# Moving the next tile's preparation two steps later inside a scan tile, in a graph network with a Mamba block

## The chip, the cores and the metric

One NeuronCore of a Trainium2 chip. Time is device microseconds of one execution of the program. TensorE multiplies matrices, VectorE, ScalarE and GpSimd do elementwise work, SyncE (SP) only issues transfers.

## The reference

With x [4096, 128] and adj [4096, 4096], all float32:

```
stage A:  for (x1, W1), (x2, W2):  h = (2 + eps) * (adj @ x_k);  three times h = relu(h @ W.T + b)
          x = layernorm(x + concat(h1, h2) @ Wm.T + bm)
stage B:  g = relu(adj @ x @ gcn_w + gcn_b);  h = layernorm(g) * ln_g + ln_b
          xc, z = split(h @ w_in);  u = silu(causal_conv(xc, 4 taps) + conv_b)
          dt_low, B, C = split(u @ w_xp);  dt = softplus(dt_low @ w_dt + b_dt)
          scan over 4096 rows, 16 states of 256 channels:  hs = exp(dt*A) * hs + dt*u*B
          y = (sum over states of hs*C + u*D) * silu(z);  out = layernorm(x + y @ w_out)
```

## The kernel before

Rows are worked in eight tiles of 512. Stage A transposes adj, multiplies it, and stores the transposed tiles 1 to 7 in HBM (`adjT`). Stage B reads them back in chunks of four 128-column blocks (`adjc`, four buffers) and multiplies each block with x: 32 "adj products" a tile, summed in one PSUM bank (`accB`), each of two instructions.

Stage B has one **window** for each tile b. A window has 16 turns, here **steps**, one for each state n. All five engines run the same steps from their own queues, written out by hand, and meet only through semaphores. In a window three things are interleaved: the scans of tile b, the **front** of tile b+1 (all that must be ready before its scans), and the **tail** of tile b−1 (gate, output projection, layernorm). Besides, TensorE works on the adj products of a tile ahead.

The scan work of step n. TensorE: spread B n+1 and spread C n−1 (a row of B or C over all partitions, in PSUM), and `sum_state(n-3)`, which adds eight transposed blocks of pr. VectorE: dBuV n (even n, L946, reads a PSUM bank), scan n−1 (L960, reads dA and dBu in SBUF), pr n−2 (L967, hs times a PSUM bank). GpSimd: dBuP n for odd n (L507, `POOL`); it waits for scan n−3 (`POOL_AFTER`), and product 1 waits for `dtu` of its tile. ScalarE: copy of a state, two dA (L714, it may be four scans ahead), the starting value of scan n−1 (L724), which the scan waits for.

The front of a tile, in order: axT (`front_ax`, ScalarE, L625); gcn (`front_gcn`, TensorE, L1123); relu (ScalarE); transpose (`front_gtr`); the statistics (`front_g`, VectorE, L886 to L895); rs and nb (`front_rs`, GpSimd, L490 and L492, tiny); hn (ScalarE, L636); transpose (`front_tr`); hT (ScalarE); eight conv products (`front_xc`, TensorE, L1143, four to each of two banks); u and sz (`front_silu`, ScalarE, L651 and L654, with a load of the activation table before and after), where sz waits for z (`front_z`, TensorE, L1152) and z for u; dbc (TensorE); bc (`front_bc`, ScalarE) and its low part `bclo` (`front_bclo`, VectorE, L900); dt product; `sp` (ScalarE), `spd`, `sp_r`, `dt` and `dtu` (VectorE, L904 to L917).

The tables at L39 to L53 say in which step of its engine each part stands: `AT` by name, `CONV` the conv products and `PLAN` the adj products of TensorE's steps, `FILL` the products that stand between the parts of front 0 before the first window, here the **gap**. `step_of` adds 1 to 16 of the names in window 0, which has no tail. Window 7 has no front, and the adj products of the kernel before end with window 5. SP issues the chunk loads in order; each waits until the chunk four before it has been multiplied. The functions that the change touches:

Of the kernel before, what the change touches and what calls it, by code (L numbers as in the profile page):

```python
# [25 lines left out]
S = 16  # L26
# [5 lines left out]
def wait(eng, sem, value):  # L32

    if not isinstance(value, int) or value > 0:
# [1 line left out]

AT = dict(pool_rs=3, pool_tail_rs=13, dve_dt=14, act_hn=4, act_hT=5, act_silu=9, act_bc=11,  # L39
          act_sp=12, act_exp=13, act_tail=14, dve_g=1, dve_bc=9, dve_sp=12, dve_gate=1, dve_tail=11, pe_tr=3,  # L40
          pe_z=7, pe_dbc=8, pe_dt=10, pe_turn=2, pe_out=9, act_b0=14, act_b1=2, act_b2=5, act_b3=9, act_ax=15, act_g=0, act_start=1, act_skip=2, act_y=4)
SHIFTED = ("pool_rs", "act_hn", "act_hT", "act_silu", "act_bc", "act_sp", "act_exp", "act_b0", "dve_g", "dve_bc", "dve_sp",
           "dve_dt", "pe_tr", "pe_z", "pe_dbc", "pe_dt")


def step_of(name, tail):

    return AT[name] + (0 if tail or name not in SHIFTED else 1)


FILL = (1, 1, 6, 1, 0, 0, 2, 9, 12)
CONV = (0, 0, 0, 0, 3, 3, 2, 0, 0, 0, 0, 0, 0, 0, 0, 0)
PLAN = (2, 4, 4, 1, 1, 0, 2, 1, 2, 1, 1, 3, 3, 2, 3, 2)  # L53
C_IN_O = (0, 2, 4, 6)
POOL = (1, 3, 5, 7, 9, 11, 13, 15)
POOL_AFTER = 3
# [4 lines left out]
def gnn_mamba(nc, x, adj, x2, eps1, eps2, W1, b1, W2, b2, Wm, bm, gcn_w, gcn_b, ln_g, ln_b, w_in, conv_w,  # L61
# [3 lines left out]
    with ctx:  # L65
# [319 lines left out]
        def _(pool):  # L385
# [114 lines left out]
            def window(b, par, tail, front):  # L500
                for n in range(S):
                    if n in POOL_B:
                        pair = nB(n) // 2
                        pool.wait_ge(b_in[pair % 2], 16 * (NPB // 4 * b + pair // 2 + 1))
                        wait(pool, scanned, S * b + (n - POOL_AFTER if n >= POOL_AFTER else -1) + 1)
                        pool.wait_ge(dtu_ready, b + 1)
                        nc.gpsimd.tensor_tensor(dBu(n, par)[:, :, 1:], dtu[par][:, :, :],  # L507
                                                b_sb[pair % 2][:, nB(n) % 2:nB(n) % 2 + 1, :].to_broadcast([P, H, TILE]),
                                                ALU.mult).then_inc(dBu_by_pool, 1)
                    if front and n == step_of('pool_rs', tail):  # L510
                        front_rs(b + 1)
                    if tail and n == AT['pool_tail_rs']:
                        tail_rs(b - 1)
# [16 lines left out]
        def _(act):  # L530
# [91 lines left out]
            def front_ax(a):  # L622
                act.wait_ge(ax1_summed, a + 1)
                wait(act, gcn_product, a)
                nc.scalar.activation(axT[:, :], accB[:, :], ACT.Copy).then_inc(ax1_ready, 1)  # L625
# [73 lines left out]
                act.dma_start(b_sb[pair % 2][:, :, :], rows_[2 * pair:2 * pair + 2, :].partition_broadcast(P))\  # L699
                    .then_inc(b_in[pair % 2], 16)  # L700

            def window(b, par, tail, front, adj_):
                for n in range(S + (0 if front else LAG)):
                    k = n - LAG
                    if k >= 0 or tail:
# [18 lines left out]
                        nc.scalar.activation(dBu(k, par)[:, :, 0], state[:, k, :], ACT.Copy).then_inc(start_set, 1)  # L724
                    if n in (AT['act_b1'], AT['act_b2'], AT['act_b3']):
                        load_B(b, par, 1 + (AT['act_b1'], AT['act_b2'], AT['act_b3']).index(n))
                    if adj_ and n == AT['act_ax']:
                        front_ax(b + 2)
                    if front:
                        if n == 1 and not tail:  # L730
                            front_ax(b + 1)
                        if n == (AT['act_g'] if tail else 2):
                            front_relu(b + 1)
                        if n == step_of('act_hn', tail):
                            front_hn(b + 1)
                        if n == step_of('act_hT', tail):
                            front_hT(b + 1)
                        if n == step_of('act_silu', tail):
                            front_silu(b + 1, 1 - par)
                        if n == step_of('act_bc', tail):  # L740
                            front_bc(b + 1, 1 - par)
                        if n == step_of('act_sp', tail):
                            front_sp(b + 1, 1 - par, 0)
                        if n == step_of('act_exp', tail):
                            front_sp(b + 1, 1 - par, 1)
                        if n == step_of('act_b0', tail):
                            load_B(b + 1, 1 - par, 0)
                    if n == AT['act_skip']:
                        skip_term(b, par)
# [20 lines left out]
            front_sp(0, 0, 0)  # L770
            front_sp(0, 0, 1)
            load_B(0, 0, 0)
            window(0, 0, False, True, True)
            window(1, 1, True, True, True)
            with act.Fori(0, 2) as i:
                window(2 * i + 2, 0, True, True, True)
                window(2 * i + 3, 1, True, True, True)
            window(6, 0, True, True, False)
            window(7, 1, True, False, False)
            tail_copy(TILES - 1)  # L780
            tail_norm(TILES - 1)

# [2 lines left out]
        def _(dve):  # L785
# [153 lines left out]
            def window(b, par, tail, front):  # L939
                for n in range(S + 2):  # L940
# [29 lines left out]
                    if tail and n == AT['dve_gate']:  # L970
                        tail_gate(b - 1, 1 - par)
                    if front:
                        if n == step_of('dve_g', tail):
                            front_g(b + 1)
                        if n == step_of('dve_bc', tail):
                            front_bclo(b + 1, 1 - par)
                        if n == step_of('dve_sp', tail):
                            front_spd(b + 1, 1 - par)
                        if 0 <= n - step_of('dve_dt', tail) < 3:
                            front_dt(b + 1, 1 - par, n - step_of('dve_dt', tail))  # L980
                    if tail:
                        if n == AT['dve_tail']:
                            tail_stats(b - 1, 1 - par)
# [23 lines left out]
        def _(pe):  # L1007
# [112 lines left out]
            def front_gcn(a):  # L1120
                pe.wait_ge(ax1_ready, a + 1)
                wait(pe, sp_abs_relu, 4 * a)
                mm(M0[:, :], gcn_w_sb[:, :], axT[:, :], start=True, stop=True).then_inc(gcn_product, 1)  # L1123
# [13 lines left out]
            def front_xc(a, j0, j1):  # L1137

                for j in range(j0, j1):
                    h, k = j // TAPS, j % TAPS  # L1140
                    if j == 0:
                        pe.wait_ge(h_ready, a + 1)
                    last = mm((M0, M1)[h][:, :], w_cv_sb[:, h, k, :], hT[:, k:k + TILE], start=(k == 0), stop=(k == TAPS - 1))  # L1143
                    if k == TAPS - 1:
                        last.then_inc(conv_summed, 1)
# [73 lines left out]
            def tail_out(b, par, groups, then):  # L1219
# [10 lines left out]
                if groups[-1] == RG - 1:  # L1230
                    last.then_inc(projected, 1)

            def window(b, par, tail, front, adj_):
                for n in range(S + 1):
                    if n % 2 and n + 1 < S:
                        spread_B(b, n + 1, par)
                    if tail and n == 0:
                        for k in LATE:
                            sum_state(b - 1, k)
                    if front and not tail and n == 1:  # L1240
                        front_gcn(b + 1)
                    if front and n == (0 if tail else 2):
                        front_gtr(b + 1)
                    if n == step_of('pe_tr', tail):
                        if adj_:
                            adj_blocks(b + 2, sum(PLAN[:n]), sum(PLAN[:n + 1]))
                        if front:
                            front_tr(b + 1)
                    if n == SUM_AFTER:
                        sum_skip(b)  # L1250
                    if n >= SUM_AFTER:
                        sum_state(b, n - SUM_AFTER)
                    if tail and 0 <= n - AT['pe_out'] < 2:
                        half = RG // 2 * (n - AT['pe_out'])
                        tail_out(b - 1, 1 - par, range(half, half + RG // 2), True)
                    if adj_ and n < S and n != step_of('pe_tr', tail):
                        adj_blocks(b + 2, sum(PLAN[:n]), sum(PLAN[:n + 1]))
                    if front:
                        k = n if tail else n - 1
                        front_xc(b + 1, sum(CONV[:max(k, 0)]), sum(CONV[:k + 1]))  # L1260
                        if n == step_of('pe_z', tail):
                            front_z(b + 1, 0)
                            front_z(b + 1, 1)
                        if n == step_of('pe_dbc', tail):
                            front_dbc(b + 1, 1 - par)
                        if n == step_of('pe_dt', tail):
                            front_dtp(b + 1, 1 - par)
                    if tail and n == AT['pe_turn']:
                        tail_turn(b - 1)
                    if adj_ and n == S:  # L1270
                        front_gcn(b + 2)
                    if n > 0:
                        spread_C(b, n - 1, par)
                    if front and n == S:
                        spread_B(b + 1, 0, 1 - par)
# [63 lines left out]
```

## Time and profile before

| | |
|---|---|
| median of 3 runs | 1144.08 us (1141.78 to 1144.95) |
| the profiled execution | 1143.51 us, its span 1141.6 us |
| busy share: TensorE, VectorE, ScalarE, GpSimd | 86%, 91%, 46%, 26% |
| mean granted TensorE clock | 0.957 |
| stage A | to about 490 us |
| gap | about 490 to 540 us |
| windows: scan 0 starts at | 529.87, 612.23, 686.97, 761.80, 836.66, 910.21, 984.2, 1057.65 us |
| last scan | 1118.7 us |

Busy is the time in which an engine had an instruction under way. A duration is that of one instruction; engines overlap the end of one with the start of the next, so that the distance of two starts is the better price of an instruction in a full queue.

### The profile page before, as it was taken

The page shows a single profiled execution, that of the slowest core. Times are in us where ns is not written, and L with a number is a line of the kernel's source. Part 1 is how long each engine was busy: PE and PEld are TensorE (multiplying, and loading weights), DVE is VectorE, ACT ScalarE, POOL GpSimd, SP SyncE. Part 2 cuts the span into 40 slices and gives each one's busy share as a digit, 9 for nine tenths or more (in the row PEclk, how much of TensorE's full clock was granted, in tenths as well). Part 3 has the DMA queues.
Part 4 walks back from the last instruction along what each step waited for, and adds up shares of the span by engine and source line. Part 5 has one row for each costly group of instructions (what it writes and reads, how often), then busy time and mean ns, then how long its engine had stood idle before and what let it go on. Part 6 is the DMA issues. An engine that isn't in the chain of part 4 may idle for free. (4 is left out here: it accounts for less than half of the span.)

```text
span 1141.6 us, 13185 instructions
## 1 busy us (share of the span) xinstructions
PE 984.3 (86%) x4162; PEld 677.3 (59%) x4162; DVE 1036.0 (91%) x858; ACT 527.2 (46%) x946; POOL 295.3 (26%) x197
## 2 busy tenths in 40 slices
PE   0689999999999999999988979979889799685555
PEld 0567777777777877444555646646556465463444
DVE  1999999999999999724999999999999999999994
ACT  1343343434444342324555555736456556564431
POOL 5321112020202110102323224332333243322340
PEclk9999999999999999999999999999999999896776
DMA  9999999999999999847444253254441542101100
GB/s 263 225 178 304 332 330 347 322 349 326 326 355 321 352 329 310 189 180 257 159 158 166 94 203 133 72 207 146 164 182 61 202 147 75 38 20 55 38 9 10
DMA packets 190908, 226.37 MB, mean 198 GB/s; under 512 B 8624, under 2 KB 164336, under 8 KB 176528
## 3 DMA queue, kind: packets, MB, share of 16 engines
q1 hardware_dynamic: 105920, 163.60, 43.9%
q10 hardware_dynamic: 81856, 54.80, 18.8%
q0 software_dynamic: 3088, 7.47, 2.1%
q8 instruction: 18, 0.29, 0.1%
q14 instruction: 26, 0.21, 0.1%
HBM read 162.66 MB, written 63.18 MB: 198 GB/s over the span
## 5 line engine op out<-in xcount | busy, mean ns | idle before, releaser
L807 DVE STREAM_TRANSPOSE at<-rows 128x1024 f32<-128x1024 f32 x136 | 267.7, 2009 | 21.6 <-DMA rows<-in_adj 8.4
L507 POOL TENSOR_TENSOR dBuP<-dtu,b_sb 128x1024 f32<-128x1024 f32 x64 | 153.5, 2398 | 397.5 <-DVE hs L960 227.5
L1025 PE MATMUL yT<-ah,xh 128*128 128x512 f32 x512 | 211.1, 412 | 47.8 <-DVE al L815 42.7
L547 ACT ACTIVATE ah<-at 128x2048 fp32r<-128x2048 f32 x64 | 122.5, 1915 | 210.2 <-PE yT L1025 208.6
L1112 PE MATMUL bank<-adjc,xm 128*128 128x512 f32 x448 | 210.7, 599 | 1.6 <-ACT axT L625 1.6
L1025 PE MATMUL yT<-ah,xl 128*128 128x512 f32 x512 | 200.5, 392 | 0.0
L1025 PE MATMUL yT<-al,xh 128*128 128x512 f32 x512 | 200.5, 392 | 0.0
L1196 PE MATMUL yT<-ident,pr 128*128 128x128 f32 x1024 | 152.5, 299 | 38.0 <-DVE pr L967 38.0
L714 ACT ACTIVATE dA<-dt,A_sb 128x512 f32<-128x512 f32 x256 | 169.7, 713 | 26.2 <-DVE dt L914 26.0
L1196 PEld LDWEIGHTS yT<-ident,pr 128*128 128x128 f32 x1024 | 132.2, 154 | 65.0 <-DVE pr L967 51.4
L967 DVE TENSOR_TENSOR pr<-hs,bank 128x1024 f32<-128x1024 f32 x128 | 153.0, 1196 | 3.9 <-PE bank L1192 3.8
L960 DVE TENSOR_TENSOR_SCAN hs<-dA,zero,dBuP 128x1026 f32<-128x1026 f32 x64 | 154.8, 2419 | 0.0
L960 DVE TENSOR_TENSOR_SCAN hs<-dA,zero,dBuV 128x1026 f32<-128x1026 f32 x64 | 151.3, 2364 | 1.7 <-DVE dBuV L946 1.2
L1025 PEld LDWEIGHTS yT<-ah,xh 128*128 128x128 f32 x512 | 96.7, 189 | 80.9 <-DVE al L815 50.7
L815 DVE TENSOR_TENSOR al<-at,ah 128x2048 fp32r<-128x2048 f32 x57 | 130.7, 2293 | 0.0
L1112 PEld LDWEIGHTS bank<-adjc,xm 128*128 128x128 f32 x448 | 80.4, 193 | 70.6 <-issue 69.6
L1025 PEld LDWEIGHTS yT<-ah,xl 128*128 128x128 f32 x512 | 96.8, 189 | 22.6 <-issue 3.6
L1025 PEld LDWEIGHTS yT<-al,xh 128*128 128x128 f32 x512 | 96.7, 189 | 21.0
L1192 PE MATMUL bank<-bc,sel 128*128 128x512 f32 x128 | 86.3, 674 | 18.3 <-DVE pr L967 16.2
L946 DVE TENSOR_TENSOR dBuV<-dtu,bank 128x1024 f32<-128x1024 f32 x64 | 77.7, 1215 | 8.1 <-PE bank L1183 7.7
L459 POOL TENSOR_TENSOR al<-at,ah 128x2048 fp32r<-128x2048 f32 x7 | 32.4, 4627 | 163.0 <-ACT ah L547 163.0
L707 ACT ACTIVATE state<-hs 128x2 f32<-128x2 f32 x128 | 25.8, 201 | 97.6 <-DVE hs L960 91.4
(150 smaller groups left out, 994.2 us busy)
## 6 DMA issues: line engine op xcount, KB each, us to landing
adjT<-at SPq DMA_DIRECT2D x56, 1024.0 KB, 7.8
adjc<-adjT SPq DMA_DIRECT2D x56, 1024.0 KB, 5.0
rows<-in_adj SPq DMA_DIRECT2D x152, 256.0 KB, 8.3
rows<-in_adj ACTq DMA_DIRECT2D x136, 256.0 KB, 8.8
b_sb<-b_dram ACTq DMA_DIRECT2D x32, 512.0 KB, 3.7
xm<-in_x SPq DMA_DIRECT2D x4, 512.0 KB, 16.2
xs<-in_L_gnn_x ACTq DMA_DIRECT2D x4, 512.0 KB, 17.1
res<-in_x POOLq DMA_DIRECT2D x8, 256.0 KB, 7.2
```

What stands on the lines that cost most here:

```text
L507: nc.gpsimd.tensor_tensor(dBu(n, par)[:, :, 1:], dtu[par][:, :, :], b_sb[pair % 2][:, nB(n) % 2:nB(n) % 2 + 1, :].to_broadcast([P, H, TILE ...
L547: nc.scalar.activation(ah[c % 2][:, :], at[c % 2][:, :, :].rearrange("p m t -> p (m t)"), ACT.Copy)\
L714: nc.scalar.activation(dA[n % NDA][:, h, 1:], dt_[par][:, h, :], ACT.Exp, scale=A_sb[:, h, n:n + 1]).then_inc(dA_ready, 1)
L807: last = nc.vector.transpose(dst.rearrange("p m (g i) -> p g m i", i=32), src.rearrange("p g (i m) -> p g m i", i=32))
L815: nc.vector.tensor_tensor(al[c % 2][:, :], at[c % 2][:, :, :].rearrange("p m t -> p (m t)"), ah[c % 2][:, :], ALU.subtract).then_inc(chunk ...
L946: nc.vector.tensor_tensor(dBuV[dve_slot(n, par)][:, :, 1:], dtu[par][:, :, :], spread_bank("B", n)[:, :].unsqueeze(1).to_broadcast([P, H, ...
L960: nc.vector.tensor_tensor_scan(flat[0], flat[1], flat[2], zero[:, :], ALU.mult, ALU.add)\
L967: nc.vector.tensor_tensor(pr[k % NPR][:, :, :], hs[k % NHS][:, :, 1:], spread_bank("C", k)[:, :].unsqueeze(1).to_broadcast([P, H, TILE]), ...
L1025: last = mm(acc[k][:, :], w[:, b, :], v[c % 2][:, cols], start=(b == 0 and j == 0), stop=(b == KB - 1 and j == 2))
L1112: last = mm(accB[:, :], xm[:, b, :], adjc[c % NADJ][:, m, :], start=(b == 0), stop=(b == KB - 1))
L1192: mm(spread_bank("C", n)[:, :], sel[:, S + n:S + n + 1].to_broadcast([P, P]), bc[par][:, :], start=True, stop=True).then_inc(C_spread, 1)
L1196: m = mm(yT[:, DI * q + P * h:DI * q + P * h + P], src[:, h, P * q:P * q + P], ident[:, :], is_transpose=True, start=first and h == 0 and ...
```

## The change

The front's places no longer differ between window 0 and the others: `step_of` and `SHIFTED` go. Nearly every part of the front moves two steps or so later (table). The adj products of tile b+2 begin in step 2 of window b, after axT of tile b+1, and their last six (`AHEAD` is 26) stand in steps 0 and 1 of window b+1, also in window 6. `FILL` ends with 6 instead of 12. axT goes from the end of the window before to ScalarE's step 4, gcn from TensorE's step 16 to step 2. Conv products are 4 and 4 in steps 7 and 8 instead of 3, 3, 2 in steps 4 to 6.

| in windows with a tail | before | after |
|---|---|---|
| TensorE: gcn, gtr, tr, z, dbc, dt | 16, 0, 3, 7, 8, 10 | 2, 3, 6, 9, 10, 11 |
| ScalarE: axT, relu, hn, hT, silu, bc, sp, exp, load of B | 15, 0, 4, 5, 9, 11, 12, 13, 14 | 4, 4, 7, 8, 10, 13, 14, 15, 15 |
| VectorE: statistics, bclo, spd, sp_r/dt/dtu | 1, 9, 12, 14/15/16 | 4, 11, 14, 15/16/17 |
| GpSimd: rs | 3 | 5 |

```diff
-          act_sp=12, act_exp=13, act_tail=14, dve_g=1, dve_bc=9, dve_sp=12, dve_gate=1, dve_tail=11, pe_tr=3,
-          pe_z=7, pe_dbc=8, pe_dt=10, pe_turn=2, pe_out=9, act_b0=14, ..., act_ax=15, act_g=0, ...)
+          act_sp=14, act_exp=15, act_tail=14, dve_g=4, dve_bc=11, dve_sp=14, dve_gate=1, dve_tail=11, pe_gcn=2, pe_gtr=3, pe_tr=6,
+          pe_z=9, pe_dbc=10, pe_dt=11, pe_turn=2, pe_out=9, act_b0=15, ..., act_ax=4, act_g=4, ...)
-FILL = (1, 1, 6, 1, 0, 0, 2, 9, 12)
-CONV = (0, 0, 0, 0, 3, 3, 2, 0, 0, 0, 0, 0, 0, 0, 0, 0)
-PLAN = (2, 4, 4, 1, 1, 0, 2, 1, 2, 1, 1, 3, 3, 2, 3, 2)
+FILL = (1, 1, 6, 1, 0, 0, 2, 9, 6)
+CONV = (0, 0, 0, 0, 0, 0, 0, 4, 4, 0, 0, 0, 0, 0, 0, 0)
+PLAN = (2, 4, 3, 2, 3, 3, 3, 0, 0, 0, 0, 2, 3, 2, 3, 2)
+AHEAD = sum(PLAN[AT['pe_gcn']:])
...
+            def adj_step(b, n, front, adj_):
+                m = AT['pe_gcn']
+                if n < m and front:
+                    adj_blocks(b + 1, AHEAD + sum(PLAN[:n]), AHEAD + sum(PLAN[:n + 1]))
+                if n >= m and adj_:
+                    adj_blocks(b + 2, sum(PLAN[m:n]), sum(PLAN[m:n + 1]))
...
-                    if front and not tail and n == 1:
+                    if front and n == AT['pe_gcn']:
                         front_gcn(b + 1)
-                    if front and n == (0 if tail else 2):
+                    if front and n == AT['pe_gtr']:
                         front_gtr(b + 1)
...
-                    if adj_ and n == S:
-                        front_gcn(b + 2)
```

## Rows read from the trace of the kernel before

**Rows 1.** The page's busy time, with the share of the span and the instructions.
```profile
PE 984.3 (86%) x4162; PEld 677.3 (59%) x4162; DVE 1036.0 (91%) x858; ACT 527.2 (46%) x946; POOL 295.3 (26%) x197
```
**Rows 2.** VectorE's waits, 548 to 1142 us: us in total, times, longest.
```profile
DVE stats L928 <- PE bank L1229: 6.5, 1, 6.5
DVE pr L967 <- PE bank L1192: 2.8, 7, 0.5
```
**Rows 3.** TensorE's timeline in the gap: start, us, what [idle before].
```profile
518.70 18.19 PE L1112 MATMUL bank<-adjc,xm 128*128 128x512 f32 x42
```
**Rows 4.** VectorE's timeline, end of the gap.
```profile
539.88 1.22 DVE L946 TENSOR_TENSOR dBuV<-dtu,bank 128x1024 f32<-128x1024 f32 x1 [7.66 <-PE bank L1183]
...
545.55 0.88 DVE L886 BATCH_NORM_STATS2 stats<-bank 128x6 f32<-128x128 f32 x4
...
550.47 1.22 DVE L946 TENSOR_TENSOR dBuV<-dtu,bank 128x1024 f32<-128x1024 f32 x1
```
**Rows 5.** GpSimd's timeline, window 0 and the first two boundaries.
```profile
530.90 5.79 POOL L507 TENSOR_TENSOR dBuP<-dtu,b_sb 128x1024 f32<-128x1024 f32 x2 [30.17 <-DMA b_sb<-b_dram]
547.26 2.98 POOL L490 TENSOR_TENSOR rs<-ve,neg_half 128x4 f32<-128x4 f32 x1 [10.57 <-DVE ve L895]
...
550.47 2.38 POOL L507 TENSOR_TENSOR dBuP<-dtu,b_sb 128x1024 f32<-128x1024 f32 x1
...
591.56 2.38 POOL L507 TENSOR_TENSOR dBuP<-dtu,b_sb 128x1024 f32<-128x1024 f32 x1 [5.66 <-issue]
611.05 2.38 POOL L507 TENSOR_TENSOR dBuP<-dtu,b_sb 128x1024 f32<-128x1024 f32 x1 [17.11 <-DMA b_sb<-b_dram]
...
684.49 2.39 POOL L507 TENSOR_TENSOR dBuP<-dtu,b_sb 128x1024 f32<-128x1024 f32 x1 [13.50 <-DVE dtu L917]
```
**Rows 6.** VectorE's timeline beside them.
```profile
551.60 3.40 DVE L960 TENSOR_TENSOR_SCAN hs<-dA,zero,dBuP 128x1026 f32<-128x1026 f32 x1
...
592.46 2.56 DVE L904 SCALAR_TENSOR_TENSOR sp_a<-dtu,sp_a 128x1024 f32<-128x1024 f32 x1
...
609.61 1.21 DVE L917 TENSOR_TENSOR dtu<-dt,u 128x1024 f32<-128x1024 f32 x1
...
612.23 3.36 DVE L960 TENSOR_TENSOR_SCAN hs<-dA,zero,dBuV 128x1026 f32<-128x1026 f32 x1
...
686.97 2.35 DVE L960 TENSOR_TENSOR_SCAN hs<-dA,zero,dBuV 128x1026 f32<-128x1026 f32 x1 [0.29 <-DVE dBuV L946]
```
**Rows 7.** TensorE's timeline, steps 7 to 9 of window 2.
```profile
717.24 1.89 PE L1152 MATMUL bank<-w_in_sb,hT 128*128 128x256 f32 x8
...
723.74 0.40 PE L1183 MATMUL bank<-bc,sel 128*128 128x512 f32 x1
723.98 1.04 PE L1196 MATMUL yT<-ident,pr 128*128 128x128 f32 x8
724.85 0.39 PE L1227 MATMUL bank<-res,ident 128*128 128x128 f32 x2
...
726.19 1.02 PE L1112 MATMUL bank<-adjc,xm 128*128 128x512 f32 x2
```
**Rows 8.** ScalarE's timeline after the silus of window 2.
```profile
719.78 1.28 ACT L656 ACT_TABLE_LOAD   x1
721.07 0.20 ACT L707 ACTIVATE state<-hs 128x2 f32<-128x2 f32 x1
...
722.41 0.19 ACT L724 ACTIVATE dBuP<-state 128x2 f32<-128x2 f32 x1
```
**Rows 9.** VectorE's timeline: two steps of window 1, scan 9 of window 2.
```profile
630.74 2.34 DVE L960 TENSOR_TENSOR_SCAN hs<-dA,zero,dBuV 128x1026 f32<-128x1026 f32 x1
...
638.78 2.35 DVE L960 TENSOR_TENSOR_SCAN hs<-dA,zero,dBuV 128x1026 f32<-128x1026 f32 x1
...
727.06 2.35 DVE L960 TENSOR_TENSOR_SCAN hs<-dA,zero,dBuP 128x1026 f32<-128x1026 f32 x1
```
**Rows 10.** Busy time by engine, granted clock, DMA share, GB/s, start of window 2.
```profile
687.00:689.00 2.00, 2.00 (x8) 1.55 (x7) 2.00 (x1) 0.32 (x2) 0.00 (x0) 0.50 0.00 0
```

More of the change, by code:

```diff
@@ L35, in wait @@
         eng.wait_ge(sem, value)
-AT = dict(pool_rs=3, pool_tail_rs=13, dve_dt=14, act_hn=4, act_hT=5, act_silu=9, act_bc=11,
-          act_sp=12, act_exp=13, act_tail=14, dve_g=1, dve_bc=9, dve_sp=12, dve_gate=1, dve_tail=11, pe_tr=3,
[L41 to L48, printed above, removed]
-FILL = (1, 1, 6, 1, 0, 0, 2, 9, 12)
-CONV = (0, 0, 0, 0, 3, 3, 2, 0, 0, 0, 0, 0, 0, 0, 0, 0)
-PLAN = (2, 4, 4, 1, 1, 0, 2, 1, 2, 1, 1, 3, 3, 2, 3, 2)
+AT = dict(pool_rs=5, pool_tail_rs=13, dve_dt=15, act_hn=7, act_hT=8, act_silu=10, act_bc=13,
+          act_sp=14, act_exp=15, act_tail=14, dve_g=4, dve_bc=11, dve_sp=14, dve_gate=1, dve_tail=11, pe_gcn=2, pe_gtr=3, pe_tr=6,
+          pe_z=9, pe_dbc=10, pe_dt=11, pe_turn=2, pe_out=9, act_b0=15, act_b1=2, act_b2=5, act_b3=9, act_ax=4, act_g=4,
+          act_start=1, act_skip=2, act_y=4)
+FILL = (1, 1, 6, 1, 0, 0, 2, 9, 6)
+CONV = (0, 0, 0, 0, 0, 0, 0, 4, 4, 0, 0, 0, 0, 0, 0, 0)
+PLAN = (2, 4, 3, 2, 3, 3, 3, 0, 0, 0, 0, 2, 3, 2, 3, 2)
+AHEAD = sum(PLAN[AT['pe_gcn']:])
 C_IN_O = (0, 2, 4, 6)
@@ L509, in window @@
                                                 ALU.mult).then_inc(dBu_by_pool, 1)
-                    if front and n == step_of('pool_rs', tail):
+                    if front and n == AT['pool_rs']:
                         front_rs(b + 1)
@@ L700, in load_B, with window @@
                     .then_inc(b_in[pair % 2], 16)
-            def window(b, par, tail, front, adj_):
+            def window(b, par, tail, front):
                 for n in range(S + (0 if front else LAG)):
@@ L726, in window @@
                         load_B(b, par, 1 + (AT['act_b1'], AT['act_b2'], AT['act_b3']).index(n))
-                    if adj_ and n == AT['act_ax']:
-                        front_ax(b + 2)
                     if front:
-                        if n == 1 and not tail:
+                        if n == AT['act_ax']:
                             front_ax(b + 1)
-                        if n == (AT['act_g'] if tail else 2):
+                        if n == AT['act_g']:
                             front_relu(b + 1)
-                        if n == step_of('act_hn', tail):
+                        if n == AT['act_hn']:
                             front_hn(b + 1)
-                        if n == step_of('act_hT', tail):
+                        if n == AT['act_hT']:
                             front_hT(b + 1)
-                        if n == step_of('act_silu', tail):
+                        if n == AT['act_silu']:
                             front_silu(b + 1, 1 - par)
-                        if n == step_of('act_bc', tail):
+                        if n == AT['act_bc']:
                             front_bc(b + 1, 1 - par)
-                        if n == step_of('act_sp', tail):
+                        if n == AT['act_sp']:
                             front_sp(b + 1, 1 - par, 0)
-                        if n == step_of('act_exp', tail):
+                        if n == AT['act_exp']:
                             front_sp(b + 1, 1 - par, 1)
-                        if n == step_of('act_b0', tail):
+                        if n == AT['act_b0']:
                             load_B(b + 1, 1 - par, 0)
@@ L772, in _ @@
             load_B(0, 0, 0)
-            window(0, 0, False, True, True)
-            window(1, 1, True, True, True)
+            window(0, 0, False, True)
+            window(1, 1, True, True)
             with act.Fori(0, 2) as i:
[L776 to L779, printed above, removed]
+                window(2 * i + 2, 0, True, True)
+                window(2 * i + 3, 1, True, True)
+            window(6, 0, True, True)
+            window(7, 1, True, False)
             tail_copy(TILES - 1)
@@ L972, in window @@
                     if front:
-                        if n == step_of('dve_g', tail):
+                        if n == AT['dve_g']:
                             front_g(b + 1)
-                        if n == step_of('dve_bc', tail):
+                        if n == AT['dve_bc']:
                             front_bclo(b + 1, 1 - par)
-                        if n == step_of('dve_sp', tail):
+                        if n == AT['dve_sp']:
                             front_spd(b + 1, 1 - par)
-                        if 0 <= n - step_of('dve_dt', tail) < 3:
-                            front_dt(b + 1, 1 - par, n - step_of('dve_dt', tail))
+                        if 0 <= n - AT['dve_dt'] < 3:
+                            front_dt(b + 1, 1 - par, n - AT['dve_dt'])
                     if tail:
@@ L1239, in window @@
                             sum_state(b - 1, k)
-                    if front and not tail and n == 1:
+                    if front and n == AT['pe_gcn']:
                         front_gcn(b + 1)
-                    if front and n == (0 if tail else 2):
+                    if front and n == AT['pe_gtr']:
                         front_gtr(b + 1)
-                    if n == step_of('pe_tr', tail):
-                        if adj_:
-                            adj_blocks(b + 2, sum(PLAN[:n]), sum(PLAN[:n + 1]))
+                    if n == AT['pe_tr']:
+                        adj_step(b, n, front, adj_)
                         if front:
@@ L1255, in window @@
                         tail_out(b - 1, 1 - par, range(half, half + RG // 2), True)
-                    if adj_ and n < S and n != step_of('pe_tr', tail):
-                        adj_blocks(b + 2, sum(PLAN[:n]), sum(PLAN[:n + 1]))
+                    if n < S and n != AT['pe_tr']:
+                        adj_step(b, n, front, adj_)
                     if front:
-                        k = n if tail else n - 1
-                        front_xc(b + 1, sum(CONV[:max(k, 0)]), sum(CONV[:k + 1]))
-                        if n == step_of('pe_z', tail):
+                        front_xc(b + 1, sum(CONV[:n]), sum(CONV[:n + 1]))
+                        if n == AT['pe_z']:
                             front_z(b + 1, 0)
                             front_z(b + 1, 1)
-                        if n == step_of('pe_dbc', tail):
+                        if n == AT['pe_dbc']:
                             front_dbc(b + 1, 1 - par)
-                        if n == step_of('pe_dt', tail):
+                        if n == AT['pe_dt']:
                             front_dtp(b + 1, 1 - par)
```

## The prediction

> **What bounds the kernel now.** I read four views in this order. The busy shares first: VectorE 91%, TensorE 86%, nothing else near [rows 1]. Shares don't say who waits for whom, so next VectorE's waits from 548 us to the end [rows 2]: in the whole scan stage it waits for TensorE's spread C rows seven times, 2.8 us in all; the 6.5 us belong to the last tile's tail, which the change leaves alone. VectorE is thus the bound of each window (a window is one scan tile, step n its n-th turn), and whatever is added to its queue or stretches an instruction of it shows in full. Third, the gap before the scans: TensorE does 21 adj products (42 instructions in 18.19 us, 0.433 each, 0.87 a product) in one piece [rows 3], and VectorE stands 7.66 us until the spread B row behind them [rows 4]. Fourth, GpSimd's and VectorE's timelines side by side [rows 5, 6], because the change moves two-operand VectorE work past GpSimd's products.
>
> **What the last view shows.** A VectorE instruction that reads two tiles in SBUF (scan, `spd`, `dt`, `dtu`) and starts while GpSimd is in a product ends late by nearly the overlap. GpSimd 611.05 to 613.43 against a scan from 612.23: overlap 1.20, the scan takes 3.36 instead of 2.35. GpSimd 550.47 to 552.85 against 551.60: overlap 1.25, scan 3.40. GpSimd 591.56 to 593.94 against `spd` at 592.46: 1.48, 2.56 instead of 1.21. So stretch = overlap less 0.15 to 0.25 [rows 5, 6]. Normally GpSimd starts at the end of a scan, and VectorE's next two are a pr product and a dBuV product, which read PSUM: nearly all the cover that its 2.38 us need.
>
> **Part (a), the gap: −5.5 us.** Six products fewer are 5.2 us; besides, step 0's two products now belong to the same tile and don't wait for axT. From rows 3, 518.70 + 15 × 0.866 = 531.7, two products 533.4, the spread (0.24, rows 7) 533.7, against 539.88 now: 6.2 earlier. From there, from start to start, dBuV takes 1.14, a scan 2.27, a pr product 1.12 (two scans, two pr and one dBuV make 7.9; rows 9 have 8.04 with a usual stretch): scan 1 at 534.85. GpSimd's second product runs 534.3 to 536.7 (530.90 + 5.79, less 2.38, rows 5), overlap 1.85, so that scan ends at 538.8; pr 0 539.95, scan 2 542.2, pr 1 543.35. C 1 is there at 542.1 (last four products end 537.4, axT taken as 1.0, gcn 0.87, three products 2.6, spread 0.24), in time. The next dBuV starts 543.35 against 550.47 [rows 4], but the statistics are still owed (545.55 until just before GpSimd's rs at 547.26: 1.56): 5.5 us gained. Bounds: 3.5 if C 1 comes 2 us late, 6.2 if nothing collides. The DMA stream is the same 32 blocks in the same order.
>
> **(b) `spd` in window 0: −1.2.** It moves from step 13, where it meets GpSimd's last product, to step 14, where it doesn't: the 1.35 stretch goes, the scan after dBuV gets its usual 0.15.
>
> **(c) Window boundaries: +5.7.** `dtu` moves from step 16 to step 17. GpSimd's product 1 waits for `dtu`. In windows 1 to 6 it now starts under pr 15 and dBuV 0, and scan 0 takes 2.35 (684.49 and 686.97). In window 0 `dtu` is already last (609.61), and that scan 0 is the 3.36 one [rows 5, 6]. After the change the other six boundaries have that order: 0.95 each.
>
> **(d) Statistics at step 4: +5.7.** At step 1 they are followed by dBuV 2, so GpSimd's pow runs beside a PSUM reader. At step 4 a scan follows at once (5 is a GpSimd state), as in window 0 now: rs takes 2.98, and the product after nb starts at 550.47, about 1.05 after the scan's end instead of at it, so it meets the following scan (3.40 against 2.35 to 2.50) [rows 5, 6]. Six windows × 0.95. Window 0 has it before and after.
>
> **(e) `bclo` to step 11: +0.6.** It gave scan 9 cover in step 9; without it that scan has the usual stretch, 0.1 × 6. Bounds of (c) to (e): nothing, where GpSimd gives way; and the whole overlaps, 1.2 + 1.2 + 0.3 a window, 16 in six. I take what the three pairs of rows show.
>
> **(f) Starting value of scan 10: +8.0.** ScalarE's step 10 now holds the silus, and they wait for z in TensorE's step 9; before, ScalarE's step 9 waited for TensorE's step 7. The value for scan n−1 is set in ScalarE's step n, behind dA n. Let T be the end of pr 4. TensorE can't pass sum 4 in step 7 before T; then come sum 4 0.87, four conv products 3.46, C 6 0.24; sum 5 0.87, four conv products 3.46, C 7 0.24; B 10 0.24, sum 6 0.87, half of the output 1.34: z starts at T + 11.65 (sum 723.98 to 724.85, output 724.85 to 726.19, spread 723.74 to 723.98, rows 7). From z's start to ScalarE free 717.24 to 721.07 = 3.83, to the end of the starting value another 1.53: T + 17.0 [rows 7, 8]. VectorE wants it after steps 7 to 10, 3.38 + 4.66 + 3.38 + 4.66 = T + 16.1 [rows 9]: 1.0 late, in windows 1 to 6. Now the value for scan 9 is there at 722.60 and scan 9 starts at 727.06, 4.5 us of cover [rows 8, 9]; one VectorE step less and two more TensorE steps use it up. TensorE's own queue reaches sum 4 earlier. From dBuV 0: it starts sum 15 at −1.0; to step 7 it has 20 products (17.3), six sums (5.2), gcn and the turn (1.7), two short transposes (0.9), ten spreads (2.4), 1.3 of waits for axT: 27.8. T is at 1.5 + 4.4 (stretched scan 0, gate) + 4.5 + 3.4 + 6.1 + 3.4 + 5.4 = 28.7. But at some boundaries TensorE runs its first 2.6 us at granted clock 0.50, the 1.2 GHz level, after it stood waiting for pr 15 [rows 10]; that costs 1.3, some 0.5 beyond the 0.9. I take three of five windows. Window 6 has no adj products after step 1, so more low clock before the conv products: 1.5. Sum 5 × 1.0 + 3 × 0.5 + 1.5 = 8.0. Bounds: 0, and 2.5 a window (15) if low clock reaches the conv products everywhere. Window 0 has no output projection (1.34 earlier): nothing.
>
> Behind the silus, in ScalarE's queue, wait dA 11, the starting values and bc; bc is there at T + 20.3, `bclo` wants it at T + 20.5. What ScalarE holds earlier (axT, relu and y at step 4, hn at step 7 until about 3.45 after the statistics) has 5 us of cover or more. `dt` at step 16: `dt` itself and two dA pairs with their copies (1.34 each, rows 8) and the value make 4.1, VectorE's own four instructions to scan 0 take 4.9: no wait. SP's queue is asked later for chunk 7 (step 11 instead of 8), ahead of the store, which goes at ScalarE's step 14 anyway: nothing; if it were late, a chunk's 5 us would have three steps of cover.
>
> The Trainium skill (ScalarE: Activation LUTs, What ACT_TABLE_LOAD costs) has a drain of about 1.38 us beside the 1.28 us load. Here the load starts at 719.78 and the next activation at 721.07, so no drain shows [rows 8]; by the page each of the six waits would be 1.4 longer, some 8 us in all.
>
> **(g) The seven C waits: −2.8.** The conv products leave steps 4 to 6 and adj products leave 7 to 10; by the same adding up C 1 to C 8 come 0.7 to 3 us early.
>
> **Sum.** −5.5 − 1.2 + 5.7 + 5.7 + 0.6 + 8.0 − 2.8 = +10.5 on the profiled execution's 1143.51 (span 1141.6 and 1.9 around it): 1154.0. The median of the timed runs is 0.6 above it; I say 1155.
>
> **Rivals.**
> 1. *TensorE is the real bound of a window*, and VectorE's stretches in steps 0 and 5 fall on slack. For it: TensorE is 86% busy over the span and full in rows 10. Then (c) to (f) cost nothing and (a), (b) and (g) stay: −9.5, 1134. It decides from the point where VectorE's idle per window exceeds the stretch, 1.9; by rows 2 it is 0.4. Chance 0.10.
> 2. *The starting value comes in time* (z 1 us earlier, or the stretches of (c) and (d) push VectorE but not T's chain): without 8.0, 1146. Against: after T both sides run free. Chance 0.14.
> 3. *No collisions*: GpSimd yields, or starts elsewhere. Without (c) to (e) and (b), and with (f) 0.3 larger a window: about 1145. Against: the same order of instructions stretched in window 0. Chance 0.13.
> 4. *The clock*: low clock through steps 0 and 1 of each window. Six products at double time are 5.2 more, less 0.9 of slack, six windows: +26 on the sum, 1180. For it: TensorE now has one product less at step 16 and waits longer there. Against: a mean clock of 0.957 leaves room for short lapses only. The Trainium skill (TensorE: Matmul & The Clock Gate, HAM oscillation) says that bursts parted by waits each start at the low clock; by that rule this is what would follow. Chance 0.05.
>
> The forecast has 0.58. A measurement of this kernel tells 0.3% (3.4 us) from no change: 1140.6 to 1147.5 is the same. Faster: rival 1 and a rest, 0.12. Same: most of 2 and 3, 0.20. Slower 0.68. The range from 1141 to 1163 holds 2 and 3, and above the sum the upper half of (f); outside lie rivals 1 and 4. The forecast's own is 1149 to 1161.
>
> **What would show it.** (a) VectorE's wait for the spread B row of 7.7 shrinks to about 1.5, and scan 1 takes about 4. (c), (d): scans 0 and 5 of windows 1 to 6 take 3.2 to 3.4. (f): one wait of VectorE's scan for ScalarE's L724 in each of windows 1 to 6, about 1 us. (g): the C waits are gone. Wrong if scans 0 and 5 stay at 2.4, or if VectorE has no wait at scan 10.

## The result, and the profile after

The changed kernel takes 1151.74 us (median of four runs, 1150.94 to 1152.94), the kernel before 1144.51 beside it: ratio 1.0073, 95% interval 1.0058 to 1.0089. It is 7.2 us slower; 10.5 had been forecast (1155). The profiled execution took 1152.26, its span 1150.3, 8.7 more than that of before. One run of those reported below (e5_b_dtu, 1217.39 us at a mean granted clock of 0.82) stands apart from all others and is left out of every comparison.

VectorE's waits after the gap, 525 us to the end (us in total, times, longest):

```profile
DVE hs L951 <- ACT dBuV L717: 8.2, 7, 1.9
DVE stats L919 <- PE bank L1220: 7.7, 1, 7.7
...
DVE dBuV L937 <- PE bank L1174: 1.5, 1, 1.5
```

The C waits (VectorE's pr product waiting for a spread C row) of [rows 2] are gone, and the wait for the spread row behind the gap's products is 1.5 us where [rows 4] has 7.66. In their place stands a new line: scan 10 waits for the starting value that ScalarE sets (L717 is L724 of before), 8.0 us of it in windows 1 to 6.

The end of the gap on VectorE, and scan 10 of windows 2 and 3:

```profile
533.52 1.22 DVE L937 TENSOR_TENSOR dBuV<-dtu,bank 128x1024 f32<-128x1024 f32 x1 [1.50 <-PE bank L1174]
534.65 3.99 DVE L951 TENSOR_TENSOR_SCAN hs<-dA,zero,dBuP 128x1026 f32<-128x1026 f32 x1
...
543.06 1.21 DVE L937 TENSOR_TENSOR dBuV<-dtu,bank 128x1024 f32<-128x1024 f32 x1
...
725.80 2.35 DVE L951 TENSOR_TENSOR_SCAN hs<-dA,zero,dBuV 128x1026 f32<-128x1026 f32 x1 [1.17 <-ACT dBuV L717]
...
802.68 2.36 DVE L951 TENSOR_TENSOR_SCAN hs<-dA,zero,dBuV 128x1026 f32<-128x1026 f32 x1 [1.89 <-ACT dBuV L717]
```

The forecast had 533.7, a scan 1 of 3.96 and a dBuV 4 at 543.35. The dBuV 4 stands at 550.47 in [rows 4].

Where the 8.7 us come from, by the start of scan 0 in each window (before: the table ahead of the prediction; after: 529.66, 605.05, 682.30, 758.33, 835.13, 911.25, 987.35, 1064.29):

| window | 0 | 1 | 2 | 3 | 4 | 5 | 6 | 7 and tail |
|---|---|---|---|---|---|---|---|---|
| before, us | 82.4 | 74.7 | 74.8 | 74.9 | 73.6 | 74.0 | 73.5 | 84.0 |
| after, us | 75.4 | 77.3 | 76.0 | 76.8 | 76.1 | 76.1 | 76.9 | 86.0 |
| difference | −7.0 | +2.5 | +1.2 | +1.9 | +2.6 | +2.1 | +3.4 | +2.1 |

The change does what it is meant to do in the gap, once, and each following window pays.

### The profile page after: what moved, and what is told of

Read it like the earlier page. It is cut to its first block and busy times, and to the rows that moved or that the text cites. A ratio compares the mean times of both kernels' runs of the same rounds, so it can differ in the third digit from the quotient of the medians.

```text
span 1150.3 us, 13181 instructions
## 1 busy us (share of the span) xinstructions
PE 995.5 (87%) x4162; PEld 684.5 (60%) x4162; DVE 1044.4 (91%) x858; ACT 528.4 (46%) x946; POOL 290.7 (25%) x197
## 5 line engine op out<-in xcount | busy, mean ns | idle before, releaser
L1103 PE MATMUL bank<-adjc,xm 128*128 128x512 f32 x448 | 208.1, 600 | 0.8 <-ACT axT L618 0.8
L1187 PE MATMUL yT<-ident,pr 128*128 128x128 f32 x1024 | 158.5, 308 | 36.0 <-DVE pr L958 35.8
L1187 PEld LDWEIGHTS yT<-ident,pr 128*128 128x128 f32 x1024 | 138.4, 160 | 65.8 <-DVE pr L958 53.3
L951 DVE TENSOR_TENSOR_SCAN hs<-dA,zero,dBuV 128x1026 f32<-128x1026 f32 x64 | 155.1, 2424 | 9.8 <-ACT dBuV L717 8.2
L951 DVE TENSOR_TENSOR_SCAN hs<-dA,zero,dBuP 128x1026 f32<-128x1026 f32 x64 | 160.1, 2502 | 0.0
L1103 PEld LDWEIGHTS bank<-adjc,xm 128*128 128x128 f32 x448 | 82.4, 194 | 79.9 <-issue 79.3
L1183 PE MATMUL bank<-bc,sel 128*128 128x512 f32 x128 | 84.5, 660 | 7.7 <-DVE pr L958 5.3
L1174 PE MATMUL bank<-bc,sel 128*128 128x512 f32 x64 | 33.6, 524 | 34.7 <-DVE pr L958 34.7
```

What stands on the lines that cost most here:

```text
L951: nc.vector.tensor_tensor_scan(flat[0], flat[1], flat[2], zero[:, :], ALU.mult, ALU.add)\
L1103: last = mm(accB[:, :], xm[:, b, :], adjc[c % NADJ][:, m, :], start=(b == 0), stop=(b == KB - 1))
L1183: mm(spread_bank("C", n)[:, :], sel[:, S + n:S + n + 1].to_broadcast([P, P]), bc[par][:, :], start=True, stop=True).then_inc(C_spread, 1)
L1187: m = mm(yT[:, DI * q + P * h:DI * q + P * h + P], src[:, h, P * q:P * q + P], ident[:, :], is_transpose=True, start=first and h == 0 and ...
```

## The experiments

All are compared with the kernel before, run on the same chip beside them. The last products of the program run at the low or the full clock by chance (a group of four on L1220 takes 1.06 or 0.61 us): VectorE's last wait (for L1220) lies between 4.9 and 8.0 us in these profiles, so that two spans can differ by 3 us for that alone. Medians and waits are read, not spans.

**Starting values earlier (e1_start).** The value for scan n is set in ScalarE's step n, ahead of that step's part of the front.

```diff
-          act_start=1, act_skip=2, act_y=4)
+          act_start=0, act_skip=2, act_y=4)
```

> The changed kernel, but each starting value is set one step earlier on ScalarE (step n for scan n instead of step n+1), so that the value for scan 10 stands ahead of the silus. My theory: VectorE's wait before scan 10 (8.0 us in windows 1 to 6) goes, but bc is three step bodies behind the silus and was just in time only because scan 10 was late; so nearly the same wait comes back before bclo, in step 11: 0.9 to 1.7 us in each window, together 6 to 8. Gain 0 to 1.5 us, about 1151. Rival (the starting value is the only thing that the silus hold back): the 8 us are gained, about 1144.

1149.72 us (1147.31 to 1151.62), ratio 1.0054 (1.0038 to 1.0069). VectorE's waits:

```profile
DVE bc L891 <- ACT bc L654: 6.2, 6, 1.2
DVE stats L919 <- PE bank L1220: 4.9, 1, 4.9
```

The waits before scan 10 are gone and six waits for bc are there, 0.9 to 1.2 us each. The rival falls: the silus hold back ScalarE's whole queue, and the next on it that VectorE needs takes over the wait. The 2.0 us gained are a little more than expected.

**And bc a step earlier (e1b_start_bc).** Besides, `act_bc=12`.

> As e1_start, and bc one ScalarE step earlier (12 instead of 13), 1.4 us. My theory: the wait before bclo shrinks to 0 to 0.3 us a window; 6 to 7.5 us gained against the changed kernel, 1144 to 1146. Rival (TensorE's steps 7 to 9 are the bound, whatever ScalarE's order is): VectorE then waits for spread C 7 to 9 instead, and the time stays at 1150 or above.

1144.35 us (1143.08 to 1147.19), ratio 1.0007 (0.9995 to 1.002): 7.4 us of the changed kernel's time are gone, and on a level with the kernel before. VectorE's longest waits:

```profile
DVE stats L919 <- PE bank L1220: 8.0, 1, 8.0
DVE yg L913 <- PE yT L1187: 2.6, 1, 2.6
DVE dBuV L937 <- PE bank L1174: 1.6, 1, 1.6
```

No wait for ScalarE is left but semaphore latencies, and TensorE's steps 7 to 9, unchanged, hold nobody.

**Statistics in step 3 (e2_stats).** `dve_g=3` in place of 4.

> The changed kernel with the statistics in VectorE's step 3 instead of 4, so that a product with a PSUM operand follows and not a scan. My theory: scan 5 of windows 0, 1 and 6 falls from 3.4 to 2.5 us; windows 2 to 5 have no such stretch and stay. 2.5 to 3 us gained, about 1149. Rival (the stretch is from something else in windows 0, 1 and 6, their unrolled code for one): scan 5 stays at 3.4 and so does the time, 1151.7.

1149.54 us (1148.45 to 1151.01), ratio 1.0051 (1.0036 to 1.0065), 2.2 less than the changed kernel. Scan 5 of window 0, here at 553.12 us and in the changed kernel at 553.84:

```profile
553.12 2.50 DVE L951 TENSOR_TENSOR_SCAN hs<-dA,zero,dBuP 128x1026 f32<-128x1026 f32 x1
```

```profile
553.84 3.40 DVE L951 TENSOR_TENSOR_SCAN hs<-dA,zero,dBuP 128x1026 f32<-128x1026 f32 x1
```

The same holds for windows 1 and 6. Windows 0, 1 and 6 still run unrolled, as in the changed kernel, so the rival falls. Part of the gain comes back before scan 10 (9.9 us of waits for ScalarE instead of 8.2), as VectorE gets there earlier, and part as three C waits of 1.3 us in all, where the changed kernel has none.

**dtu in step 16 (e3_dtu).** `dve_dt=14` in place of 15.

> The changed kernel with sp_r, dt and dtu in steps 14, 15, 16 instead of 15, 16, 17. My theory: GpSimd's product 1 starts a pr product earlier and is out of the way of scan 0: scan 0 of windows 1 to 7 takes 2.35 instead of 2.9 to 3.3. 4.3 us less on the scans (window 1's too, which the kernel before has), less up to 0.6 given back at scan 10: 3.5 to 4.5 gained, about 1148. Rival (the overlap costs nothing by itself, VectorE waits for TensorE or ScalarE anyway): no gain, 1151.7.

1154.03 us (1152.42 to 1156.98), ratio 1.0088 (1.0072 to 1.0104): 2.3 us slower than the changed kernel, where 4 us less were expected. VectorE, boundary of windows 1 and 2:

```profile
683.66 2.35 DVE L951 TENSOR_TENSOR_SCAN hs<-dA,zero,dBuV 128x1026 f32<-128x1026 f32 x1 [0.29 <-ACT dBuV L717]
685.94 1.20 DVE L913 TENSOR_TENSOR yg<-yT,sz 128x1024 f32<-128x1024 f32 x1
...
691.35 1.22 DVE L958 TENSOR_TENSOR pr<-hs,bank 128x1024 f32<-128x1024 f32 x1 [0.72 <-PE bank L1183]
...
696.14 1.22 DVE L958 TENSOR_TENSOR pr<-hs,bank 128x1024 f32<-128x1024 f32 x1 [1.31 <-PE bank L1183]
```

The mechanism is right (scan 0 falls to 2.35) and the price is not: 7.8 us of waits for TensorE's C rows, mostly C 0 and C 1. With `dtu` last, TensorE may begin its sum of pr 15 one instruction (1.1 us) sooner, and VectorE is held at scan 0 meanwhile: at the boundary of windows 1 and 2 the sums start 4.4 us before scan 0 in the changed kernel, 3.0 us before it here. I had counted that head start in TensorE's favour in step (f) and forgot it here. The waits before scan 10 grow too, from 8.0 to 9.7 us in windows 1 to 6.

**With a lighter step 2 (e3b_plan).** e3_dtu, and

```diff
-PLAN = (2, 4, 3, 2, 3, 3, 3, 0, 0, 0, 0, 2, 3, 2, 3, 2)
+PLAN = (2, 4, 1, 2, 3, 3, 3, 0, 0, 0, 0, 2, 3, 3, 3, 3)
```

> As e3_dtu (which came out 2.3 us slower than the changed kernel: its scans 0 fell to 2.35 us as expected, but nine waits for spread C 0 and C 1 of 7.8 us took their place), with two adj products fewer in TensorE's step 2 and one more in steps 13 and 15. My theory now: dtu as last instruction also lets TensorE begin its sums 1.1 us earlier, and VectorE's stretched scan 0 gives it 0.6 more; without both, steps 0 to 2 are too full for C 1. Two products are 1.7 us: the C 1 waits go (5 us), the C 0 waits stay (0.6 to 0.7 in some windows). 1148 to 1150. Rival (low clock at the boundary makes the C waits, not the count of products): they stay at 5 us or more, 1153 to 1155.

1148.77 us (1145.06 to 1149.85), ratio 1.0042 (1.0026 to 1.0058), 5.3 less than e3_dtu. VectorE's waits for C:

```profile
DVE pr L958 <- PE bank L1183: 0.9, 2, 0.7
```

So two products fewer are enough, and the rival's number is out. But the clock has its part: the C waits go with the clock that TensorE was granted in the 2.5 us after scan 0. Windows 2 and 3 of e3_dtu (the columns are PE, PEld, DVE, ACT, POOL busy, then the granted clock):

```profile
683.66:686.16 2.50, 2.50 (x6) 1.34 (x6) 2.50 (x2) 0.11 (x1) 0.06 (x1) 0.55 0.00 0
761.75:764.25 2.50, 2.50 (x7) 1.17 (x7) 2.50 (x2) 0.11 (x1) 0.06 (x1) 1.00 0.00 0
```

In front of C 0 both kernels have the same products, and its wait goes with this clock alone: 0.65 to 0.73 us at 0.50 to 0.57, 0.39 at 0.64, 0.17 and 0.21 at 0.77 and 0.76, none from 0.87 up, over the six windows of each. In front of C 1 both count: in e3_dtu its wait is 1.2 to 1.4 us in the four windows at 0.55 to 0.76 and 0.58 in window 3 at 1.00 (window 6 has no adj products after step 1, and none). In e3b_plan C 1 isn't waited for at any clock. No run changes the clock by itself.

**The boundary alone (e5_b_dtu).** The kernel before with `dve_dt=15` in every window.

> The kernel before with one part of the change alone: sp_r, dt and dtu in steps 15 to 17 in every window (in window 0 they are there already). My theory: scan 0 of windows 2 to 6 takes 2.96 instead of 2.35, that of window 7 3.3, together 4.0 us more; the C waits of 2.8 us go, because TensorE starts 1.1 earlier against VectorE; net 1 us, 1145 to 1146. Rival (the collision costs what it lasts, and C waits are another matter): 4 us slower, 1148.

1145.78 us (median of eleven runs, 1144.52 to 1147.23; 1145.88 with the twelfth), ratio 1.002 (1.0009 to 1.003). Scans 0 take 2.97 (windows 2 to 5), 2.93 and 3.29. The C waits from 525 us to the end fall to 1.5 us, from 3.8 in the kernel before ([rows 2] start at 548 us and so leave out one of 1.0):

```profile
DVE pr L967 <- PE bank L1192: 1.5, 2, 1.0
...
DVE dBuV L946 <- DVE dtu L917: 0.4, 2, 0.2
```

The boundary's order costs 4.0 us on the scans and 0.9 on dBuV 0, which now starts behind `dtu`; 2.3 come back from the C waits. That leaves 2.6, and the ratio gives 2.3. It is e3_dtu's trade from the other side. The rival's 1148 is out.

**The cures together (e8_best1).** `act_start=0`, `act_bc=12`, `dve_g=3`.

> The changed kernel with the two cures that worked: starting values a step earlier and bc in ScalarE's step 12 (1144.35 together), and statistics in step 3 (2.2 us by itself). My theory: the parts add up, no wait before scan 10 and bclo, scan 5 at 2.5 us in every window: 1141 to 1142.5, 2 to 3 us under the kernel before. Rival (the statistics' 0.9 us come back as a wait for bc in the same windows, as they partly did at scan 10 in e2_stats, 1.7 us): 1143.5 to 1144.5.

1143.05 us (1140.49 to 1145.05), ratio 0.9995 (0.9985 to 1.0004): level with the kernel before, between the two expectations. bc isn't waited for; four C waits of 1.9 us in all, two of them in window 6, have taken part of the gain, so the rival named the wrong wait but the right size.

**All of it (e9_best2).** e8_best1, `dve_dt=14`, the lighter PLAN, and `bclo` after the tail's statistics.

> As e8_best1, with dtu in step 16, the lighter step 2 of e3b_plan, and bclo behind the tail's statistics in step 11. My theory: scans 0 at 2.35 us (4.3 less), C 0 waits of 1 to 2 us in all: 1138 to 1140. Rival (TensorE bounds steps 0 to 9 once VectorE's stretches are gone; with all VectorE stretches away it waits for C 0 to C 8): C waits of 4 us or more and 1142 or above.

1140.44 us (1138.87 to 1141.08), ratio 0.9969 (0.9956 to 0.9981). The C waits are 6.0 us, more than my 1 to 2, 3.6 of them at C 0: TensorE is now the nearer bound of steps 0 and 1. Once more, beside the next:

> e9_best2 once more, beside e10_best3 on the same chip, for a firm comparison: 1139 to 1141, 3 us under the kernel before. Rival (the first result was a matter of the chip): within 1 us of the kernel before.

1138.78 us (1138.49 to 1140.45), ratio 0.9959 (0.9945 to 0.9972).

**One product less in step 0 (e10_best3).**

```diff
-FILL = (1, 1, 6, 1, 0, 0, 2, 9, 6)
+FILL = (1, 1, 6, 1, 0, 0, 2, 9, 7)
-PLAN = (2, 4, 1, 2, 3, 3, 3, 0, 0, 0, 0, 2, 3, 3, 3, 3)
+PLAN = (1, 4, 1, 2, 3, 3, 3, 0, 0, 0, 0, 3, 3, 3, 3, 3)
```

> As e9_best2 (1140.4, with waits of 0.6 to 0.7 us for spread C 0 in windows 2 to 6), with one adj product fewer in TensorE's step 0, one more in step 11 and one more in the gap (7 instead of 6, 0.87 us). My theory: the C 0 waits of 3.3 us go, 0.9 come back in the gap: 2 to 2.5 us gained, 1138 to 1138.5. Rival (VectorE's saved time only moves the wait to C 7 and C 8 in steps 8 and 9, since TensorE's queue is full there): no gain, 1140 to 1141.

1133.65 us (1132.99 to 1135.99), ratio 0.9914 (0.99 to 0.9928): 10.2 us under the kernel before and 5.1 under e9_again, twice the forecast. VectorE's waits of e9_again and of this one:

```profile
DVE stats L919 <- PE bank L1220: 7.8, 1, 7.8
DVE pr L958 <- PE bank L1183: 4.4, 10, 0.7
...
DVE dBuV L937 <- PE bank L1174: 2.4, 4, 1.6
```

```profile
DVE stats L919 <- PE bank L1220: 6.4, 1, 6.4
...
DVE dBuV L937 <- PE bank L1174: 1.6, 1, 1.6
DVE pr L958 <- PE bank L1183: 1.4, 2, 0.8
```

3.8 us of waits for TensorE in the windows are gone, and the last wait is 1.4 shorter, which may be chance. The 0.9 us that I expected back in the gap don't show: VectorE's wait for the spread B row is 1.62 in both, since the product added to the gap is the one taken from step 0, and both stand ahead of that row. But this profile is 1.0 us later already at 511 us, ahead of the added product. 3.8 + 1.4 − 1.0 is 4.2 of the 5.1 between the spans; the rest is open.

**The control (e7_b_start).** The kernel before with `act_start=0`.

> The kernel before, with each starting value set a step earlier on ScalarE, as in e1_start: a control. My theory: in the kernel before, the value of scan 9 lies ready 4.5 us early, so that nothing waits for it: no change, 1143 to 1145. Rival (setting the values earlier is a gain anywhere, for instance by what it frees on ScalarE): 2 us or more faster.

1143.21 us (1141.75 to 1145.09), ratio 0.9993 (0.9984 to 1.0002): no change, although its profile has C waits of 5.9 us instead of 3.8. Setting the values earlier helps only where they are late.

## Why the prediction was right, point by point

| step | forecast | in the trace |
|---|---|---|
| (a), (b) window 0 | −6.7 | −7.0 |
| (c) scan 0 | +5.7 | +4.0: 0.62 in windows 2 to 5, 0.57 and 0.94 |
| (d) scan 5 | +5.7 | +1.8: 0.9 in windows 1 and 6, nothing in 2 to 5 |
| (e) other scans | +0.6 | about +1.1 |
| (f) scan 10's value | +8.0 | +8.0 |
| (g) C waits | −2.8 | −2.8 |
| dBuV 0 behind `dtu` | 0 | about +1.6 |
| scan 4 behind the statistics | 0 | about +0.7 |
| last tile's tail | 0 | +1.2 |
| sum | +10.5 | +8.6 of 8.7 |

(The two "about" rows and (e) are from windows 1, 2 and 4 counted instruction by instruction: `dtu` to dBuV 0 0.20 to 0.28 longer, the end of the statistics to scan 4 up to 0.14 longer, the other scans 0.2. Over all six boundaries `dtu` to dBuV 0 is 0.16 to 0.53 longer.)

**(f) was right in mechanism and size.** ScalarE after the silus of window 2:

```profile
722.86 1.28 ACT L649 ACT_TABLE_LOAD   x1
724.15 0.20 ACT L700 ACTIVATE state<-hs 128x2 f32<-128x2 f32 x1
724.26 1.32 ACT L707 ACTIVATE dA<-dt,A_sb 128x512 f32<-128x512 f32 x2
725.49 0.19 ACT L717 ACTIVATE dBuV<-state 128x2 f32<-128x2 f32 x1
```

TensorE, sum 4 and z of the same window:

```profile
708.72 1.09 PE L1187 MATMUL yT<-ident,pr 128*128 128x128 f32 x8
...
720.31 1.89 PE L1143 MATMUL bank<-w_in_sb,hT 128*128 128x256 f32 x8
```

From sum 4 to z 11.6 us (forecast 11.65, but its own terms add up to 11.59), from z to ScalarE free 3.84 (3.83), to the end of the starting value 725.68, T + 16.96 (17.0). VectorE's six waits are 1.07, 1.17, 1.89, 1.26, 1.17 and 1.39; the forecast had two of 1.0, three of 1.5 (low clock) and 1.5 for window 6. So the total is right and its spread over the windows only roughly: with 11.59 the forecast's 1.0 would have been 0.9, and among windows 1 to 5 one stands out, not three (window 3, 1.89, with the lowest granted clock in the 2.5 us after scan 0: 0.79, the others 0.86 to 1.00). The load starts at 722.86 and the next activation at 724.15: no drain shows here either, against the Trainium skill (ScalarE: Activation LUTs, What ACT_TABLE_LOAD costs). e1_start and e1b_start_bc show the wait by itself: moving the value leaves 6.2 us at bc, moving both leaves nothing.

**(d) is the mis-sized term, 3.9 too much.** I took one pair of rows, from window 0, for six windows. My own sign of being wrong, that scan 5 stays at 2.4, came true in windows 2 to 5, where it takes 2.43 to 2.45. GpSimd behind the statistics of window 2, and of window 6:

```profile
700.61 1.01 POOL L483 TENSOR_TENSOR rs<-ve,neg_half 128x4 f32<-128x4 f32 x1 [4.89 <-DVE ve L886]
701.69 1.25 POOL L485 TENSOR_TENSOR nb<-mr,rs 128x4 f32<-128x4 f32 x1
703.03 2.38 POOL L500 TENSOR_TENSOR dBuP<-dtu,b_sb 128x1024 f32<-128x1024 f32 x1
```

```profile
1005.71 3.04 POOL L483 TENSOR_TENSOR rs<-ve,neg_half 128x4 f32<-128x4 f32 x1 [4.90 <-DVE ve L886]
1008.83 0.20 POOL L485 TENSOR_TENSOR nb<-mr,rs 128x4 f32<-128x4 f32 x1
1008.98 2.36 POOL L500 TENSOR_TENSOR dBuP<-dtu,b_sb 128x1024 f32<-128x1024 f32 x1
```

VectorE beside them:

```profile
700.36 0.16 DVE L886 TENSOR_SCALAR ve<-mv 128x4 f32<-128x4 f32 x1
700.59 2.36 DVE L951 TENSOR_TENSOR_SCAN hs<-dA,zero,dBuV 128x1026 f32<-128x1026 f32 x1
...
705.11 2.44 DVE L951 TENSOR_TENSOR_SCAN hs<-dA,zero,dBuP 128x1026 f32<-128x1026 f32 x1
...
1005.47 0.16 DVE L886 TENSOR_SCALAR ve<-mv 128x4 f32<-128x4 f32 x1
1005.60 2.35 DVE L951 TENSOR_TENSOR_SCAN hs<-dA,zero,dBuV 128x1026 f32<-128x1026 f32 x1
...
1010.11 3.38 DVE L951 TENSOR_TENSOR_SCAN hs<-dA,zero,dBuP 128x1026 f32<-128x1026 f32 x1
```

In window 6 the scan is 0.11 us under way when rs starts, rs lasts until 0.80 after the scan's end, and product 7 starts 1.03 after that end and meets scan 5. In window 2 the scan starts 0.10 later behind the statistics (0.23 after `ve` instead of 0.13) and rs only 0.02 after the scan. Then rs gets through in 1.01, its time everywhere else, only nb is held until the scan's end, and the product starts 0.08 after it, beside PSUM readers. Windows 2 to 5, which the program runs as a loop, have the second order; windows 0, 1 and 6 the first. The trace shows the two orders; that it is the 0.1 us that decides between them was not tested by itself. e2_stats takes both away and takes 0.9 off scan 5 of windows 0, 1 and 6.

**(c) was right in mechanism, 1.7 too much.** The boundary of windows 1 and 2, GpSimd and VectorE:

```profile
680.74 2.38 POOL L500 TENSOR_TENSOR dBuP<-dtu,b_sb 128x1024 f32<-128x1024 f32 x1 [15.77 <-DVE dtu L908]
```

```profile
682.30 2.97 DVE L951 TENSOR_TENSOR_SCAN hs<-dA,zero,dBuV 128x1026 f32<-128x1026 f32 x1 [0.29 <-DVE dBuV L937]
```

Overlap 683.12 − 682.30 = 0.82, stretch 0.62: the rule "overlap less 0.2" holds, but in the loop's windows scan 0 waits 0.29 for dBuV, which [rows 6] show too, at 686.97, and I didn't subtract it from the overlap. e5_b_dtu isolates (c): the same 2.97, but only 2.3 us net, as its C waits fall by 2.3. e3_dtu shows the other side of that trade: the order that stretches scan 0 also gives TensorE its head start.

**(a), (b), (g)** came as worked out, to 0.3 us. The rows not forecast are small waits: a dBuV 0 straight behind `dtu` starts 0.2 to 0.5 us late, six times, and the last tile's tail took 1.2 more, which may be the clock of its products. Over- and underestimates cancel in part: with (c) and (d) right and the last three rows left out the forecast would have been 1149.4, with them 1152.9. That 1155 lies within 3.3 us of the 1151.74 measured is in part luck.

**The rivals.** (1) TensorE as the real bound: no, there is no C wait left, and the stretches show in full. It is what the kernels without the stretches ran into, though (e3_dtu 7.8, e9_best2 6.0). (2) and (3) fell: 8.0 us of waits and stretched scans. (4) The clock: the mean is 0.944 against 0.957. In the 2.5 us before scan 0 of windows 1 to 6 the granted clock is 0.50 to 0.84 (before: 0.50 to 1.00), in the next 2.5 us 0.79 to 1.00, and then 1.00. Steps 0 and 1 don't double, and TensorE is in time for every C. The Trainium skill's rule (TensorE: Matmul & The Clock Gate, HAM oscillation), that a burst after a wait starts at the low clock, agrees with these lapses; they are too short for the rival's price. In e3_dtu, without the head start, they do reach VectorE.

## What to carry to other kernels

Moving the next tile's preparation later pays once, in the gap, and costs in every tile whatever it makes late or collide; count the second part per tile and per queue. Where an instruction waits in an in-order queue, everything behind it waits: list what the bound engine needs from behind it, because moving the first such item only uncovers the next (8.0 us at the starting value, then 6.2 at bc, then none). And when a stretch on the bound engine is removed, look at what the next engine did with it: with the stretches and the ScalarE waits gone, TensorE's steps 0 and 2 had to be lightened as well (e3b_plan, e10_best3) for the gain to show in full: 1138.78 (e9_again) and 1133.65 (e10_best3) against 1143.89.

## What the runs showed of the hardware that was not expected

- `rs`, a 128x4 operation on GpSimd that takes 1.01 us in every other place, took 3.04 when it started 0.11 us into a scan. Started 0.02 us into the scan it took its 1.01, and `nb` behind it (0.20 by itself) took 1.25, until the scan's end. With the one order the next 2.38 us product starts 1.03 us after the scan's end, with the other 0.08; what decides between the two orders was not tested by itself.
- A scan that starts inside a GpSimd product ends late by the overlap less 0.2 (3.99, 3.40, 3.29 and 2.97 for 2.35), while a dBuV or pr product, which reads PSUM, keeps its 1.2 beside the same products. The Trainium skill (GPSIMD Engine Reference, Specifications) has the SBUF interfaces shared between the two engines, with contention for VectorE instructions of two SBUF inputs; this trace agrees with the kinds of instruction.
- The last tile's wait for its output products is 4.9 to 8.0 us in the profiles of kernels that do the same there.
